# Token-shift mix of a mixture-of-experts stage: two of GpSimd's five elementwise operations per tile made by VectorE

## What is computed

```python
# end of block 1: one expert of 8 per batch, then a square product
h = gelu(y @ w1 + b1)                  # 512 -> 1024, w1, w2 of the batch's expert
z = h @ w2 + b2                        # 1024 -> 512
x1 = x + y + 0.3 * (z @ Wo + bo)
# start of block 2: mix of each row with the row before it in its batch
xprev = concatenate([shift_state[:, None, :], x1[:, :-1]], axis=1)
dxprev = xprev - x1
xk = x1 + dxprev * time_maa_k          # key rows, scattered into a buffer by expert
xr = x1 + dxprev * time_maa_r          # receptance rows
r = sigmoid(xr @ w_recept)
```

## Time and profile before

| | us |
|---|---|
| median of 3 runs | 2650.61 |
| lowest, highest | 2650.34, 2656.22 |
| the profiled execution | 2650.74 |
| its span, first to last instruction | 2649.1 |
| TensorE busy in the span | 2490.9 (94%) |
| VectorE, ScalarE, GpSimd busy | 1139.7, 899.0, 556.9 |
| mean granted TensorE clock | 0.974 of full |

### The profile page before, as it was taken

How to read it: one execution, slowest core, us unless ns; L and a number is a source line. 1 busy time by engine, 2 the same in 40 slices (tenths; PEclk the granted TensorE clock), 3 DMA queues, 4 the chain that set the end, 5 groups by cost and what they waited for, 6 DMA issues and landing times. The chain is left out here.

```text
span 2649.1 us, 42201 instructions
## 1 busy us (share of the span) xinstructions
PE 2490.9 (94%) x12550; PEld 2061.2 (78%) x12552; DVE 1139.7 (43%) x1735; ACT 899.0 (34%) x1451; POOL 556.9 (21%) x498
## 2 busy tenths in 40 slices
PE   8999999996999659999999969999969999999999
PEld 4777888885888548888888859999968888888876
DVE  4545444442322234434344426676643333333356
ACT  2333333333544312222222225666643222222233
POOL 1100000002222136657666630000001111111100
PEclk9999999998999879999999989999989999999999
DMA  7776888875755273345435336666641111111035
GB/s 285 231 256 243 287 285 283 285 271 209 269 182 168 87 286 116 108 155 206 118 107 190 99 127 236 233 228 237 227 173 41 32 32 32 32 28 28 24 100 169
DMA packets 137488, 444.26 MB, mean 168 GB/s; under 512 B 30562, under 2 KB 33058, under 8 KB 118352
## 3 DMA queue, kind: packets, MB, share of 16 engines
q1 hardware_dynamic: 109760, 340.68, 37.5%
q0 software_dynamic: 18736, 60.80, 7.6%
q10 hardware_dynamic: 8928, 41.98, 4.1%
HBM read 676.15 MB, written 161.58 MB: 316 GB/s over the span
## 5 line engine op out<-in xcount | busy, mean ns | idle before, releaser
L814 POOL DMA_INDIRECT s_x<-in_x_rows,route x72 | 70.1, 973 | 706.7 <-POOLq L123 509.3
L87 PE MATMUL s_g<-wx_hi,s_x_hi 128*128 128x512 f32 x512 | 206.3, 403 | 6.6 <-DVE s_x_lo L1847 4.0
L89 PE MATMUL s_g<-wx_hi,s_x_lo 128*128 128x512 f32 x512 | 201.1, 393 | 0.0
L88 PE MATMUL s_g<-wx_lo,s_x_hi 128*128 128x512 f32 x512 | 200.5, 392 | 0.0
L1581 DVE TENSOR_TENSOR s_w_lo<-s_w_raw,s_w_hi 128x1024 fp32r<-128x1024 f32 x128 | 151.0, 1222 | 68.0 <-ACT s_w_hi L1533 66.4
L87 PE MATMUL s_g<-s_w_hi,s_c_hi 128*128 128x512 f32 x384 | 152.4, 397 | 0.0
L87 PE MATMUL s_h_ps<-s_x_hi,s_w_hi 128*128 128x256 f32 x512 | 146.1, 285 | 6.4 <-DVE s_w_lo L1581 6.4
L89 PE MATMUL s_g<-s_w_hi,s_c_lo 128*128 128x512 f32 x384 | 149.7, 390 | 0.0
L88 PE MATMUL s_g<-s_w_lo,s_c_hi 128*128 128x512 f32 x384 | 149.3, 389 | 0.0
L88 PE MATMUL s_h_ps<-s_x_lo,s_w_hi 128*128 128x256 f32 x512 | 146.1, 285 | 0.0
L89 PE MATMUL s_h_ps<-s_x_hi,s_w_lo 128*128 128x256 f32 x512 | 146.0, 285 | 0.0
(11 more groups left out here) (342 smaller groups left out, 6832.2 us busy)
## 6 DMA issues: line engine op xcount, KB each, us to landing
s_half<-mid_w ACTq DMA_DIRECT2D x128, 2048.0 KB
s_w<-mid_rw SPq DMA_DIRECT2D x72, 2048.0 KB
s_w_raw<-in_w SPq DMA_DIRECT2D x64, 512.0 KB, 5.8
mid_w<-s_x_grp SPq DMA_DIRECT2D x32, 1024.0 KB, 4.8
mid_w<-s_pool_b SPq DMA_DIRECT2D x32, 1024.0 KB, 4.8
s_w_raw<-in_w1h SPq DMA_DIRECT2D x16, 2048.0 KB, 8.5
s_w_raw<-in_w2h SPq DMA_DIRECT2D x16, 2048.0 KB, 7.7
mid_routed<-s_o_sb SPq DMA_DIRECT2D x72, 256.0 KB
```

Source lines behind the costliest of these rows:

```text
L87: pe.matmul(out, a_hi, w_hi, start=first, stop=False, skip_group_check=True)
L88: pe.matmul(out, a_hi, w_lo, start=False, stop=False, skip_group_check=True)
L89: return pe.matmul(out, a_lo, w_hi, start=False, stop=last, skip_group_check=True)
L814: pool.indirect_dma_start(x[:, i % NI], None, ins["x_rows"], bass.IndirectOffsetOnAxis(idx[:, i:i + 1].bitcast(U32), 0)).then_inc(S[f"x_in ...
```

## The change

GpSimd's `mix` keeps `dx`, the `maa_k` product, `xk` and the scatter. The two operations for `xr` go to a new VectorE step `mix_r` with lag 3, between `z_lo` and `combine`. It waits for GpSimd's `dx`, multiplies into `xr`, waits for that (semaphore `r_part`), and adds `x1` in place. GpSimd's `dx` now waits until VectorE has read the `dx` before it, and VectorE's `x1` waits for `xr` of the tile before.

```diff
             def mix(i, n, turn):
                 pool.wait_ge(S["prev_in"], i * 48 + 48)
+                wait_for(pool, S["r_part"], i)
                 pool.tensor_tensor(dx[:], prev[:], x1[:], ALU.subtract).then_inc(S["dx"], 1)
                 pool.wait_ge(S["dx"], i + 1)
-                pool.tensor_tensor(k_part[:], dx[:], maa_r[:], ALU.mult).then_inc(S["r_part"], 1)
-                pool.wait_ge(S["r_part"], i + 1)
-                wait_for(pool, S["txr"], i)
-                pool.tensor_tensor(xr[:], k_part[:], x1[:], ALU.add).then_inc(S["xr"], 1)
-                pool.wait_ge(S["xr"], i + 1)
                 pool.tensor_tensor(k_part[:], dx[:], maa_k[:], ALU.mult).then_inc(S["k_part"], 1)
...
                 wait_for(dve, S["xk"], i)
+                wait_for(dve, S["xr"], i)
                 wait_for(dve, S["x1_out"], i * 16)
                 dve.scalar_tensor_tensor(x1[:], square_ps[:], 0.3, base[:, n], ALU.mult, ALU.add).then_inc(S["x1"], 1)
+
+            def mix_r(i, n, turn):
+                dve.wait_ge(S["dx"], i + 1)
+                wait_for(dve, S["txr"], i)
+                dve.tensor_tensor(xr[:], dx[:], maa_r[:], ALU.mult).then_inc(S["r_part"], 1)
+                dve.wait_ge(S["r_part"], i + 1)
+                dve.tensor_tensor(xr[:], xr[:], x1[:], ALU.add).then_inc(S["xr"], 1)
...
             software_pipeline(dve, NB, [
-                (2, z_add), (1, h_add(0)), (2, part_lo(z_lo, tz_ps, z_hi, "z_hi", "z_lo")), (0, combine), (1, h_add(1)),
+                (2, z_add), (1, h_add(0)), (2, part_lo(z_lo, tz_ps, z_hi, "z_hi", "z_lo")), (3, mix_r), (0, combine), (1, h_add(1)),
```

## The result

| | before | changed |
|---|---|---|
| median of 17 runs each, us | 2653.97 | 2660.47 |
| lowest, highest | 2650.34, 2660.32 | 2657.44, 2663.55 |
| the profiled execution | 2650.74 | 2659.11 |
| its span | 2649.1 | 2657.4 |
| VectorE, GpSimd busy | 1139.7, 556.9 | 1179.1, 472.2 |

The changed kernel takes 1.0023 times as long, with a 95% interval of 1.0016 to 1.0031: about 6.1 us slower (the two medians differ by 6.5). That is within the 0.3% which the prediction counted as no change, but it is a loss, since the interval lies wholly above 1. The median lies 1.5 us above the predicted range (to 2659.0), and the sum had +1.3. The profiled executions differ by 8.4 us, their spans by 8.3.

The account below looks back on a forecast made before the run. The prediction took TensorE as the bound, busy 557.77 of 559.00 us. From the profiled 2650.74 us, ordinary turns 0, two late turns 0 and the last tile +1.3 gave 2652.0 us, range 2648.5 to 2659.

Parts of the forecast that it names:

- the sum: Whole kernel: ordinary turns 0, two late turns 0, last tile +1.3 us on the profiled 2650.74, giving 2652.0 us.
- What bounds the stage: TensorE, 990 to 1549 us: busy 557.77 of 559.00 us, so at most 1.2 us to gain; waits for `s_h`.
- Ordinary turns at 0: VectorE's pair delays the second gelu by 1.34 us, within TensorE's 1.47 us spare, leaving 0.29: no cost.
- The late turns at 0: Two turns behind a change of expert: 0 taken, between -0.6 us and +1.6 us each.
- Contention: Late turns: VectorE operations with two SBUF inputs and GpSimd operations reading SBUF exclude each other; `mix_r` beside the key operations.
- the upper bound: Late turn with contention: VectorE's sum ends about 1200.6, `h_pre` starts at 1202.1 instead of 1200.53, +1.6 us for TensorE.
- `s_shared`: Late turns, lower bound: `mix_r` fits into the 1.40 us in which `y_part` waits for this transfer anyway.
- The last tile at +1.3: End of the stage: VectorE's `xr` contends with GpSimd, its sum ending by 1564.4: +1.3 us; without contention -0.3.
- Rival 1: Ordinary turns: the spare before the second half's transposes does not hold; one collision per turn +17 us, 2669; chance 0.08.
- Rival 2: Late turns: the new wait for `dx` bites if `prev` comes later; at 3 us twice, 2658; chance 0.07.
- Rival 3: End of the stage: paced by the scatter and gets shorter, about -2 us, 2648.6; chance 0.06.
- rival 4: Whole kernel: nothing moves beyond 0.3 us, VectorE getting its inputs first in the last tile; 2650.5; chance 0.15.

Follow-up runs that it names:

- no_key_ops: The changed kernel with GpSimd's key product and sum made for the first tile only; ratio 1.0002 to the kernel before.
- before_shared_first: The kernel before, with SyncE's load of `s_shared` put ahead of the `prev` transfers and the store of `x1`; ratio 0.9989.
- before_weights_mid: The kernel before, with ScalarE's issue of the second weights one step later, behind the second `ht_hi`; ratio 1.0010.
- both: The changed kernel with `mix_r` behind the first half's `ht_lo` and the second weights issued at the end of ScalarE's turn; ratio 1.0009 to the kernel before.
- behind_shared_first: The changed kernel with `mix_r` behind the first half's `ht_lo` and `s_shared` loaded ahead of `prev` and the `x1` store; ratio 0.9999 to the kernel before.
- key_after_xr: The changed kernel with GpSimd waiting for VectorE's `xr` before its key product; ratio 1.0100 to the kernel before.
- before_wait_only: The kernel before, with VectorE waiting for `dx` ahead of `y_part` and no operation added; ratio 1.0000.
- shared_first: The changed kernel with SyncE's load of `s_shared` put ahead of the `prev` transfers and the store of `x1`; ratio 1.0038 to the kernel before.
- change_again: The changed kernel as it is, profiled and measured a second time; ratio 1.0021 to the kernel before.
- weights_mid: The changed kernel with ScalarE's issue of the second weights one step later, behind the second `ht_hi`; ratio 1.0033 to the kernel before.
- before_work_only: The kernel before, with a product and a sum on constants added on VectorE ahead of `y_part`, without the wait for `dx`; ratio 1.0050.
- r_behind_ht: The changed kernel with `mix_r` moved behind the first half's `ht_lo`, ahead of `x1`; ratio 1.0008 to the kernel before.

## Why the prediction was wrong

The sign of the sum was right, its size and range were not: +1.3 forecast, about +6.1 measured by ratio, 8.3 in the span.

- **What bounds the stage: right.** TensorE had 1.2 us to give, and it lost 3.6 in two waits, where the prediction looked for them.
- **Ordinary turns at 0: right**, to 0.1 us: `h_pre` 3.38 us behind `z_lo` (3.46 forecast), mostly 0.33 to 0.46 us spare (0.29 forecast), product and sum 0.68 and 0.69 us, no wait.
- **The late turns at 0, with ends of -0.6 and +1.6 each: the step that failed.** They cost +3.69 and +3.01. Three errors add up in it. *Contention* was priced rightly by the upper bound (product 1.79 and sum 1.67; +1.42 in the second turn, where it is alone) but then was not taken, on the reasoning that an issue of the weights level with `prev` would let `prev` land sooner. It was issued level (1183.09 and 1182.95), and `dx` ended 0.14 us behind `z_lo` where it had been 0.17: no gain. *`s_shared`* was taken as landing where it did. It landed 3.0 us later relative to `z_lo`; that made 0.7 us more in the first turn, and without any contention (`no_key_ops`) it still leaves a wait of 1.86 us in place of 0.63. The prediction had the row, as a wait of 1.40 us in which the pair would be hidden, and had the later issue of the weights it stands behind, and didn't join them; that issue explains only a part of the 3.0, and the rest stays open. *The clock* was not priced: 1.57 and 1.54 us of half clock behind the waits, nearly as much as the growth of the waits (2.11 and 1.42).
- **The last tile at +1.3: wrong in size and sign of the tile, by 1.6 us.** VectorE was first by 0.04 us: -0.3. What did cost 1.5 us there is half clock in the last square product. That stretch shows at the same place in 10 of the 16 profiles. `before_shared_first` and `before_weights_mid` have it, without the pair on VectorE; `both` and `behind_shared_first` have the pair and lack it. So it isn't the pair's doing, and 1.5 of the 8.3 us between the two spans may be no part of what the change costs.
- **Rival 1** (a collision every turn) did not happen; its price was shown by `key_after_xr`. **Rival 2** (the wait for `dx`) was not it (`before_wait_only` 1.0000) though its price was shown by `shared_first`: against the changed kernel `dx` ends 4.0 us later relative to `z_lo`, and TensorE's wait is 3.2 us longer, with the 0.67 for `s_shared` gone. **Rival 3** and **rival 4** did not happen: the stage's end was still paced by `xr` and `r`, and things moved.

The balance of the spans: contention 2 x 1.4, `s_shared` 0.7, clock 2 x 1.55 and 1.54, last tile -0.3 come to 7.9; less the 0.48 by which `z_lo` of the last tile came sooner than the two turns' sum (6.70 and 6.22) it is 7.4 at the start of the next stage's transfers. The 8.3 of these two spans and the 6.1 by the ratio are apart at least in part because single executions of the kernel before scatter from 2650.34 to 2660.32, and the profiled one lies near the lowest. The balance is that of two profiles; `change_again` repeats its waits and its three stretches at half clock.

## What to carry to other kernels

Follow a delay past the consumer that you are watching: the same engine that waits for it may issue a large transfer, and a small one that stands behind it comes late in the very turn that has no spare. Count on no rate for that; here one issue 1.24 us later went with a landing 3.0 us later, another 2.93 us later with 1.3. Where two transfers and a contention meet in one rare turn, take the upper bound unless a row shows the relief, and add to a wait of TensorE what the matmuls behind it lose at half clock. An operation put where its inputs are just ready is put where the engine that made them starts its next one; behind the last link of the chain it may take three times as long and cost nothing.

## What the runs showed of the hardware that was not expected

- **Half clock behind short waits.** Waits of TensorE of 2.75 and 2.04 us (changed), 2.88 and 2.31 (again), 2.66 and 3.10 (`weights_mid`), and one of 1.86 (`no_key_ops`) were followed by a granted clock of 0.50, that is 1.2 GHz, in a stretch of some 3.4 us; it costs 1.4 to 1.6 us (4.73 to 4.85 from one group of transposes to the next, for 3.27 to 3.30). The wait's length alone doesn't decide it: the clock stayed at 1.00 behind 1.90 us in `before_work_only`, and behind 2.40 us in `r_behind_ht` the matmuls came at the full clock (0.39 us for one of 0.63):

```profile
1203.77 0.66 PE L1413 MATMUL s_th_ps<-ident,s_h 128*128 128x128 f32 x4 [2.40 <-ACT s_h L1267]
...
1204.50 0.39 PE L88 MATMUL s_th_ps<-wo_lo,s_xr_hi 128*128 128x512 f32 x1
```

In the last square product it fell behind the waits of 0.79 and 1.41 us that had left it at 1.00 in the kernel before. What decides stays open.
- **One VectorE operation held up to the end of a GpSimd addition that started after it**: 2.47 us for 0.69. The gather beside it is not enough, since in eight turns of `r_behind_ht` the product takes 0.68, in four of them beside a gather; what goes with the long ones is an addition of GpSimd that starts 0.56 to 0.66 us behind the product, just before it would end. In `behind_shared_first` the ordinary turns alternate: 2.42 to 2.45 us where the addition starts 0.57 to 0.60 behind, 0.68 where it starts 0.67 or more behind.
- **Who is held up can turn on 0.04 us.** In the late turns GpSimd began 0.04 us ahead of VectorE (1196.42 and 1196.46) and VectorE's product took 1.79; at the last tile VectorE began at 1568.18, GpSimd at 1568.22, and GpSimd's took 1.81. But the start alone does not decide, as the point before this one shows: there the product started 0.6 us ahead and ended last.
